# State-space stage: both SiLUs as Tanh, +1 and a GpSimd product, spread over the steps with the exponentials of delta

## The reference, cut to what matters

```python
xz = jnp.einsum('bld,ed->ble', xn, in_proj_w)
xi, z = jnp.split(xz, 2, axis=-1)
xc = conv(xi.transpose(0, 2, 1), conv_w) + conv_b      # 4 taps, per channel
u = jax.nn.silu(xc.transpose(0, 2, 1))
x_dbl = jnp.einsum('bld,ed->ble', u, x_proj_w)
dt, Bm, Cm = jnp.split(x_dbl, [DT_RANK, DT_RANK + D_STATE], axis=-1)
delta = jax.nn.softplus(jnp.einsum('blr,dr->bld', dt, dt_proj_w) + dt_proj_b)
dA = jnp.exp(delta_t[..., None] * A)                   # at each position t
dBu = (delta_t * u_t)[..., None] * B_t[:, None, :]
h = dA * h + dBu
y = jnp.einsum('bds,bs->bd', h, C_t)                   # end of the scan over t
y = (ys.swapaxes(0, 1) + u * D_param) * jax.nn.silu(z)
out = jnp.einsum('ble,de->bld', y, out_proj_w)
```

## Time and profile before

| | us |
|---|---|
| median of 3 runs | 4052.83 |
| lowest and highest | 4045.92, 4057.39 |
| the profiled execution | 4050.71 |
| its span, first to last instruction | 4048.8 |
| busy: TensorE, VectorE, ScalarE, GpSimd | 3284.8, 2608.9, 1731.4, 1379.1 |

### The profile page before, as it was taken

The page is one execution under the profiler, slowest core; times in us unless marked ns, Lnnn a source line. Parts: engine busy times, 40 slices in busy tenths (PEclk is TensorE's granted clock), DMA queues, the critical chain, the costliest instruction groups (busy, mean ns, idle before and its releaser), DMA issues. The chain is left out here.

```text
span 4048.8 us, 55788 instructions
## 1 busy us (share of the span) xinstructions
PE 3284.8 (81%) x16504; PEld 1863.2 (46%) x16505; DVE 2608.9 (64%) x5013; ACT 1731.4 (43%) x3367; POOL 1379.1 (34%) x1394
## 2 busy tenths in 40 slices
PE   4888888888669889797988899776597787997595
PEld 1333333333236544444444456454375475664364
DVE  2899898888957576674757577785144864223235
ACT  3666656566335346365455555112032332222022
POOL 2787777777700020202011000442534100001633
PEclk9999899999979879899898999887798998998798
DMA  2545455445500000000000000900233794000236
GB/s 89 138 131 133 121 133 135 125 130 134 129 22 1 15 1 2 2 2 2 2 2 1 2 1 1 241 2 6 89 103 118 182 136 59 16 10 0 94 92 200
DMA packets 370274, 283.12 MB, mean 70 GB/s; under 512 B 214026, under 2 KB 290366, under 8 KB 370016
## 3 DMA queue, kind: packets, MB, share of 16 engines
q1 hardware_dynamic: 356960, 246.43, 24.5%
q0 software_dynamic: 13056, 33.65, 2.4%
HBM read 205.69 MB, written 76.16 MB: 70 GB/s over the span
## 5 line engine op out<-in xcount | busy, mean ns | idle before, releaser
L436 POOL TENSOR_TENSOR mamba_dBu<-mamba_du,mamba_bcs 128x512 f32<-128x512 f32 x512 | 640.7, 1270 | 227.6 <-DMA mamba_bcs<-mamba_bc 187.7
L384 PE MATMUL mamba_banks<-mamba_hc,ident 128*128 128x512 f32 x1024 | 540.1, 640 | 166.6 <-DVE mamba_hc L633 166.2
L1427 DVE TENSOR_REDUCE attn_mp<-attn_banks 128x1 f32<-128x512 f32 (+3 forms) x768 | 381.8, 550 | 96.4 <-PE attn_banks L1150 54.5
L579 ACT ACTIVATE mamba_banks<-mamba_delta,mamba_a_neg 128x512 f32<-128x512 f32 x512 | 352.1, 691 | 198.8 <-DVE mamba_hc L633 189.7
L384 PEld LDWEIGHTS mamba_banks<-mamba_hc,ident 128*128 128x128 f32 x1024 | 183.7, 198 | 483.6 <-DVE mamba_hc L633 361.6
L626 DVE TENSOR_TENSOR_SCAN mamba_banks<-mamba_banks,mamba_dBu 128x512 f32<-128x512 f32 x256 | 312.2, 1219 | 96.2 <-POOL mamba_dBu L436 57.8
L633 DVE TENSOR_TENSOR mamba_hc<-mamba_banks,mamba_bcs 128x512 f32<-128x512 f32 x512 | 344.2, 674 | 24.5 <-PE mamba_banks L384 24.5
L626 DVE TENSOR_TENSOR_SCAN mamba_banks<-mamba_banks,mamba_h_end,mamba_dBu 128x512 f32<-128x512 f32 x256 | 327.2, 1278 | 34.4 <-ACT mamba_banks L579 24.1
L1147 PE MATMUL attn_banks<-attn_kT,attn_qT 96*128 96x512 bf16 (+3 forms) x768 | 273.4, 372 | 10.7 <-ACT attn_kT L1316 5.0
L1335 ACT ACTIVATE attn_probs<-attn_banks 128x512 f32<-128x512 f32 (+1 forms) x384 | 182.1, 528 | 180.5 <-PE attn_banks L1166 155.8
L1163 PE MATMUL attn_banks<-attn_qT,attn_kT 98*128 98x512 bf16 (+3 forms) x768 | 248.6, 339 | 10.2 <-ACT attn_probs L1335 5.3
(11 more groups left out here) (382 smaller groups left out, 6539.7 us busy)
## 6 DMA issues: line engine op xcount, KB each, us to landing
mamba_bcs<-mamba_bc SPq DMA_DIRECT2D x256, 512.0 KB
moe_slots_moe<-moe_pad SPq DMA_DIRECT2D x2, 9252.0 KB, 56.2
moe_xg<-moe_slots_moe SPq DMA_DIRECT2D x144, 128.5 KB
mix_qkv<-mixA_qkv SPq DMA_DIRECT2D x8, 1536.0 KB, 5.9
mixA_y<-moe_rows SPq DMA_DIRECT2D x16, 512.0 KB, 6.1
mix_qk<-mix_qkv SPq DMA_DIRECT2D x16, 512.0 KB, 7.3
mix_v<-mix_qkv SPq DMA_DIRECT2D x16, 256.0 KB, 7.4
mix_out<-mixB_oh SPq DMA_DIRECT2D x16, 256.0 KB, 7.5
```

The lines of the kernel that those rows point to most:

```text
L384: pe.matmul(banks[:, SUMS + k % PAIR, :], c.ident[:, :], hc[:, n % RING, :], start=False, stop=True, skip_group_check=True).then_inc(sem(" ...
L436: pool.tensor_tensor(dBu[:, n % RING, :], du[:, v, k, :], bcs[:, i_of(n) % 4, 0, :], ALU.mult)\
L579: act.activation(banks[:, n % RING, :], delta[:, v, k, :], ACT.Exp, scale=a_neg[:, k, st:st + 1])\
L1427: dve.tensor_reduce(mp[:, qt // GT, j, qt % GT, at // 512:at // 512 + 1], banks[:, item % SLOTS, 0:size], AX.X, ALU.max).then_inc(sem("rin ...
```

## The change

- SiLU of u: the copy of the convolution out of PSUM becomes (a + bias) / 2 (Identity with a per-partition operand `half_bias`, made once on VectorE). Tanh into `th_u` and a pass that adds 1 follow on ScalarE, block by block at steps 35, 38, 41, 44; GpSimd multiplies (`silu_u`) at 37, 40, 43, 45.
- SiLU of z: the copy halves. Tanh and +1 (`tanh_z`) at 10, 12, 16, 20 on ScalarE, the product (`silu_z`, now GpSimd's) at 12, 16, 20, 24. `th_u` and `th_z` have two buffers each, so a Tanh waits for the product two blocks before.
- The copy of dt, B and C moves from 52 to 51, Abs and Relu from 54 to 57 to 52, 54, 56, 58, the four Exp from 58 to 53, 55, 57, 59, the Ln from 59 to 60.

```diff
--- before.py
+++ after.py
...
-TURNED_AT, XI_COPY_AT, CONV_COPY_AT, U_AT, Z_COPY_AT, XD_AT, RELU_AT, EXP_AT, LN_AT = 20, (23, 25, 27, 29), (33, 36, 39, 42), 44, (46, 47, 48, 49), 52, (54, 55, 56, 57), 58, 59
-SILU_Z_AT = 10
+TURNED_AT, XI_COPY_AT, CONV_COPY_AT, U_AT, Z_COPY_AT, XD_AT, RELU_AT, EXP_AT, LN_AT = 20, (23, 25, 27, 29), (33, 36, 39, 42), (35, 38, 41, 44), (46, 47, 48, 49), 51, (52, 54, 56, 58), (53, 55, 57, 59), 60
+TANH_Z_AT, SILU_Z_AT, SILU_U_AT = (10, 12, 16, 20), (12, 16, 20, 24), (37, 40, 43, 45)
...
+        half_bias = s.sb("half_bias", [P, CB])
+        th_u, th_z = s.sb("th_u", [P, 2, GN]), s.sb("th_z", [P, 2, GN])
...
+                def silu_u(g, v, k):
+
+                    pool.wait_ge(sem("gate_u"), g * CB + k + 1)
+                    pool.tensor_tensor(u[:, v, k, :], th_u[:, k % 2, :], u[:, v, k, :], ALU.mult)\
+                        .then_inc(sem("u_ready"), 1)
+
+                def silu_z(g, v, i):
+
+                    pool.wait_ge(sem("gate_z"), g * CB + i + 1)
+                    pool.tensor_tensor(sz[:, v, i, :], th_z[:, i % 2, :], sz[:, v, i, :], ALU.mult)\
+                        .then_inc(sem("sz_ready"), 1)
...
+                        if n in SILU_Z_AT:
+                            silu_z(g, v, SILU_Z_AT.index(n))
+                        if after and n in SILU_U_AT:
+                            silu_u(g + 1, 1 - v, SILU_U_AT.index(n))
...
+                for k in range(CB):
+                    silu_u(0, 0, k)
...
-                        act.copy(u[:, v, k, :], banks[:, FRONT + k % 2, :]).then_inc(sem("conv_copied"), 1)
-                    if n == U_AT:
-                        for k in range(CB):
-                            act.wait_ge(sem("conv_copied"), g * CB + k + 1)
-                            act.activation(u[:, v, k, :], u[:, v, k, :], ACT.Silu, bias=chan[:, k, 4:5]).then_inc(sem("u_ready"), 1)
+                        act.activation(u[:, v, k, :], banks[:, FRONT + k % 2, :], ACT.Identity, bias=half_bias[:, k:k + 1], scale=0.5)\
+                           .then_inc(sem("conv_copied"), 1)
+                    if n in U_AT:
+                        k = U_AT.index(n)
+                        act.wait_ge(sem("conv_copied"), g * CB + k + 1)
+                        if not (first and k < 2):
+                            act.wait_ge(sem("u_ready"), g * CB + k - 1)
+                        act.activation(th_u[:, k % 2, :], u[:, v, k, :], ACT.Tanh).then_inc(sem("tanh_u"), 1)
+                        act.wait_ge(sem("tanh_u"), g * CB + k + 1)
+                        act.activation(th_u[:, k % 2, :], th_u[:, k % 2, :], ACT.Identity, bias=1.0).then_inc(sem("gate_u"), 1)
...
-                        act.copy(sz[:, v, i, :], banks[:, FRONT + i % 2, :]).then_inc(sem("z_copied"), 1)
+                        act.activation(sz[:, v, i, :], banks[:, FRONT + i % 2, :], ACT.Identity, scale=0.5).then_inc(sem("z_copied"), 1)
...
-                    if n == EXP_AT:
-                        for k in range(CB):
-                            act.wait_ge(sem("abs_ready"), g * CB + k + 1)
-                            act.activation(ex[:, k, :], ex[:, k, :], ACT.Exp, scale=-1.0).then_inc(sem("exp_ready"), 1)
+                    if n in EXP_AT:
+                        k = EXP_AT.index(n)
+                        act.wait_ge(sem("abs_ready"), g * CB + k + 1)
+                        act.activation(ex[:, k, :], ex[:, k, :], ACT.Exp, scale=-1.0).then_inc(sem("exp_ready"), 1)
...
-                def silu_z(g, v):
-
-                    for i in range(CB):
-                        act.wait_ge(sem("z_copied"), g * CB + i + 1)
-                        act.activation(sz[:, v, i, :], sz[:, v, i, :], ACT.Silu).then_inc(sem("sz_ready"), 1)
+                def tanh_z(g, v, before, i):
+
+                    act.wait_ge(sem("z_copied"), g * CB + i + 1)
+                    if before or i >= 2:
+                        act.wait_ge(sem("sz_ready"), g * CB + i - 1)
+                    act.activation(th_z[:, i % 2, :], sz[:, v, i, :], ACT.Tanh).then_inc(sem("tanh_z"), 1)
+                    act.wait_ge(sem("tanh_z"), g * CB + i + 1)
+                    act.activation(th_z[:, i % 2, :], th_z[:, i % 2, :], ACT.Identity, bias=1.0).then_inc(sem("gate_z"), 1)
...
-                        if n == SILU_Z_AT:
-                            silu_z(g, v)
+                        if n in TANH_Z_AT:
+                            tanh_z(g, v, before, TANH_Z_AT.index(n))
...
+                act.wait_ge(sem("bias_halved"), 1)
...
+                dve.tensor_scalar(half_bias[:, :], chan[:, :, 4], 0.5, None, ALU.mult).then_inc(sem("bias_halved"), 1)
```

2 lines of the change are left out of this document (1 added, 1 removed).

## The result

The changed kernel takes 4035.0 us (median of 7 runs, 4026.3 to 4040.3), the kernel before 4053.1 beside it: ratio 0.9949, 95% interval 0.9937 to 0.9961. The forecast was 4011, its range 3988 to 4032. The direction is right; the gain is 18 us by the medians (21 by the ratio) instead of 42, and the time lies 3 us above the range.

What follows compares the result with a forecast made beforehand. VectorE was taken to bound the state-space stage, so only its idle time could be won. Terms of 17.7 + 14 + 6.75 + 3.3 = 41.8 us, against the 4052.8 median, gave 4011 us; range 3988 to 4032.

Steps and rivals of the forecast that it cites:

- Term 1: Step 10 of the groups: SiLU of z in short pieces removes VectorE's idle time at scan 11; -17.7 us.
- Terms 2 and 3: Steps 44 to 61: earlier TensorE work, less a new wait at scan 53; -14 us even groups, -6.75 odd groups.
- Term 4: Prologue before the first scan: projection goes on earlier and a table load goes; -3.3 us.
- GpSimd at nothing: GpSimd in the state-space stage: eight added products a group, 9.8 us, fit its slack and cost 0 us.
- Rival A: Dense GpSimd stretches: late B and C loads are passed on, 1 us each in eight groups; 4027 us, chance 0.14.
- B: State-space stage: GpSimd becomes the bound, its eight added products show, 69 us in seven groups; 4080 us, chance 0.07.
- Rival C: Scan 53: no stall since TensorE is less behind, 3 us return in seven groups; 3990 us, chance 0.08.
- Table loads: ScalarE in the state-space stage: 17 loads instead of 49; 32 fewer with the prologue, worth 41 us of ScalarE.

Runs made afterwards that it cites:

- adds_late: Changed kernel with VectorE's two adds to x at steps 14 and 16 (from 12 and 14), TensorE's next transposes at 16 (from 14); 3932.2 us, ratio 0.9904.
- u_only: Kernel before with only the SiLU of u changed; SiLU of z and the steps of delta as before; 4032.4 us, ratio 0.9941.
- relu_back: Changed kernel with Abs and Relu back at steps 54 to 57, the Exp burst at 58, Ln at 59; 3940.4 us, ratio 0.9922.

## Why the prediction was wrong

**The sum for the stage was 41.8; 30.7 came.** By its own terms:

*Term 1, -17.7 forecast, about -8.4 measured (17.7 less 9.3 of new waits); this is the step that failed inside the stage.* The idle time at scan 11 went in all groups, as the walk of ScalarE said. What I left out is who stood behind it. While VectorE waited 2.83 us for ScalarE, TensorE caught up with the output projection, and the adds to x at 12 and 14 found it ready (0.2 us of waits in seven groups). Without the stall the adds wait themselves: 0.50 and 1.06 in group 2, 9.5 us in all. The prediction even took these adds as slack ("the two adds that VectorE makes at 12 and 14 give 1.2 more"). The rows to see it by were there: four passes in 1.72 us, so two sums and an output part of 8 half-size passes make 2.58 us a step against VectorE's 1.715. Walking TensorE through steps 8 to 14, as it was walked through 44 to 52, would have shown it. adds_late tests this by itself: moved two steps back, the adds cost nothing, and the stage takes 998.9 us, that is 38.4 less than before, where terms 1 to 3 make 38.5. That they meet within 0.1 us is luck in part: stages of one program differ by 1 to 4 us.

*Terms 2 and 3, -20.75 forecast, about -19.3 measured* (27.7 of the stage less the 8.4; with the 1.7 us behind the last scan taken out they would be 21.0). The places came as written: waits of 3.02 and 2.86 at scan 53 (forecast 3.2 and 2.9), 2.86 and 1.02 at scan 61 (3.6 and 1.25), no wait at scan 45, the copies of z no longer late. Not foreseen was a wait of about 1.3 us at scan 36 of even groups, where ScalarE has the two copies of the sums and then the Tanh pair of step 35 ahead of decay 36.

*Term 4, -3.3 forecast, -3.0 measured*: first scan at 84.8, forecast 84.4 (83.3 to 85.2 in the other undelayed profiles with the new SiLU of u).

*GpSimd at nothing*: 3.7 us of waits for it in eight groups beyond the first one, at steps 27 to 44 of groups 2 and 4, behind late loads of B and C. Rival A, 16 us, didn't come, nor B: a product of the new ones costs 1.28 us, and GpSimd still waited 85.4 us for its data.

*Rival C* had a true core and a wrong size. C thought of a TensorE less far behind, and the wait at 53 came as forecast. It can be avoided by another order (u_only and relu_back have none), but relu_back gives 3.9 us for it and not 20, since the last burst takes the rest back.

*Table loads*: 17, as the order said. By the Trainium skill (ScalarE: Activation LUTs, What ACT_TABLE_LOAD costs) the 32 loads taken out would have been worth 85 us of ScalarE, an estimate from its 2.66 us a switch, twice the 41 of the rows. Each load still takes 1283 ns with 0.1 us of idle time before eight of them, so the trace after shows no drain either, and the price of the rows stands.

**Behind the stage the prediction had nothing, and there the second part of the miss lies.** I set the whole gain of the stage equal to the gain of the kernel. A loss behind it was a term at nothing, without a reason given. On chips C and D the changed kernel has 0.9932 and 0.9930, 27 to 28 us of its 30.7 (25 and 30 by the medians); in the first measurement and on A 0.9949 and 0.9941, 21 to 24 (18 both times by the medians). The scatter of the clock's dips, up to 9 us, and the stops in the last expert stage of chip A lie between. With the first term at 8.4 the sum would have been 32.5 and the forecast 4020; the other 15 us up to the measured 4035 are the loss behind the stage. Either miss alone would have left the time inside the range (4020 with the first, 4026 with the second); it took both. What share of the second belongs to the change stays open. A term with a size it could not have had, but the profile of before showed 113.5 us in which ScalarE waited for nothing named, in the two expert stages, and waits of that kind belonged into the range: its upper end stood 3 us too low.

## What to carry to other kernels

When a stall is taken out, walk every engine through the steps that it covered, not only the one that caused it: here TensorE used ScalarE's stall to catch up, and the consumer of its output took half of that term's gain back as a new wait. Moving the consumer two steps later brought the stage's whole sum, 38.4 us. And before a stage's gain is booked as the kernel's, look in the later stages for waits with no releaser and for dips of the granted clock; here they moved the 30 us that one profiled execution could show by up to 16.
